# A conv + GRU kernel on one core: ScalarE copies gate biases into PSUM in place of VectorE's bias additions, and the tap shift products are issued in halves of 128 columns

## What is computed

```
x = x + (depthwise_causal_conv(x, taps = cond[:, None, :]) + b)
x = x + gru_scan(h0 = cond, inputs = x)         # 64 steps, hs stacked on the time axis
# one GRU step, h and x_t are 128 x 512, W_* are 512 x 1536
gi = x_t @ W_ih + b_ih ;  gh = h @ W_hh + b_hh  # each split in r, z, n
r = sigmoid(i_r + h_r) ;  z = sigmoid(i_z + h_z)
n = tanh(i_n + r * h_n)
h = (1 - z) * n + z * h
```

## Time and profile before

| | us |
|---|---|
| the executions shown | 1250.62 and 1250.66, median 1250.64 |
| span of the profiled execution, first to last instruction | 1249.1 |
| median less span (start and end outside the instructions) | 1.5 |
| TensorE busy | 1207.4 (97%) |
| VectorE busy | 663.6 (53%) |
| ScalarE busy | 343.1 (27%) |

### The profile page before, as it was taken

The page is one execution under the profiler, slowest core; times in us unless marked ns, Lnnn a source line. Parts: engine busy times, 40 slices in busy tenths (PEclk is TensorE's granted clock), DMA queues, the critical chain, the costliest instruction groups (busy, mean ns, idle before and its releaser), DMA issues.

```text
span 1249.1 us, 14699 instructions
## 1 busy us (share of the span) xinstructions
PE 1207.4 (97%) x5508; PEld 1019.2 (82%) x5508; DVE 663.6 (53%) x1015; ACT 343.1 (27%) x474; POOL 16.0 (1%) x20
## 2 busy tenths in 40 slices
PE   5499989999999999999999999999999999999998
PEld 5499978888888888888888888888888888888886
DVE  5255685555555455555555555555555555555554
ACT  6266661212212122212221211222121212122111
POOL 1000040000000000000000000000000000000000
PEclk9699999999999999999999999999999999999999
DMA  9996758222112222221222222122222211222200
GB/s 189 208 265 214 160 159 270 51 51 51 46 38 42 50 50 50 50 46 38 42 50 50 50 50 47 38 41 50 50 50 50 47 39 40 50 50 50 50 18 18
DMA packets 247730, 92.55 MB, mean 74 GB/s; under 512 B 203168, under 2 KB 236704, under 8 KB 246432
## 3 DMA queue, kind: packets, MB, share of 16 engines
q1 hardware_dynamic: 246848, 91.45, 31.9%
q10 hardware_dynamic: 864, 0.85, 0.3%
HBM read 58.72 MB, written 33.55 MB: 74 GB/s over the span
## 4 chain that ended last, share of the span: by engine, by line
PE 94%; DMA 4%; ACT 1%; POOL 0%; DVE 0%; SPq 0%; issue 0%; ACTq 0%; DVEq 0%
PE bank L715 83%; PE bank L695 9%; DMA x_sb<-in_x_dram 4%; PE bank L704 2%; ACT w_ih_hi L513 1%; ACT w_hh_hi L513 0%; POOL w_hh_lo L297 0%; DVE stage L578 0%; SPq L328 0%; DVE h_less_n L646 0%; DVE h L648 0%; DVE pre_z L640 0%; ACTq L317 0%; SPq L312 0%; ACT xT_hi L505 0%
## 5 line engine op out<-in xcount | busy, mean ns | idle before, releaser
L715 PE MATMUL bank<-w_ih_hi,xT_hi 128*128 128x512 f32 x768 | 305.5, 398 | 1.3 <-DVE w_ih_lo L297 1.1
L715 PE MATMUL bank<-w_hh_hi,hT_hi 128*128 128x512 f32 x768 | 298.9, 389 | 1.2 <-DVE w_hh_lo L297 0.8
L715 PE MATMUL bank<-w_ih_hi,xT_lo 128*128 128x512 f32 x768 | 300.0, 391 | 0.0
L715 PE MATMUL bank<-w_ih_lo,xT_hi 128*128 128x512 f32 x768 | 299.3, 390 | 0.0
L715 PE MATMUL bank<-w_hh_hi,hT_lo 128*128 128x512 f32 x768 | 298.8, 389 | 0.0
L715 PE MATMUL bank<-w_hh_lo,hT_hi 128*128 128x512 f32 x768 | 298.8, 389 | 0.0
L715 PEld LDWEIGHTS bank<-w_hh_hi,hT_hi 128*128 128x128 f32 x768 | 144.2, 188 | 31.8 <-issue 1.9
L715 PEld LDWEIGHTS bank<-w_ih_hi,xT_hi 128*128 128x128 f32 x768 | 144.3, 188 | 30.9 <-POOL w_ih_lo L297 1.0
L715 PEld LDWEIGHTS bank<-w_ih_hi,xT_lo 128*128 128x128 f32 x768 | 144.1, 188 | 31.0
L715 PEld LDWEIGHTS bank<-w_hh_hi,hT_lo 128*128 128x128 f32 x768 | 144.2, 188 | 29.9
L715 PEld LDWEIGHTS bank<-w_hh_lo,hT_hi 128*128 128x128 f32 x768 | 144.2, 188 | 29.9
(11 more groups left out here) (54 smaller groups left out, 796.6 us busy)
## 6 DMA issues: line engine op xcount, KB each, us to landing
xt<-xres SPq DMA_DIRECT2D x128, 128.0 KB, 2.6
out_dram<-out_t SPq DMA_DIRECT2D x64, 256.0 KB, 2.1
x_quads<-xres SPq DMA_DIRECT2D x252, 64.0 KB, 2.4
x_sb<-in_x_dram SPq DMA_DIRECT2D x2, 4096.0 KB, 35.3
xres<-kept SPq DMA_DIRECT2D x4, 1920.0 KB, 9.1
x_sb<-in_x_dram SPq DMA_DIRECT2D x2, 3072.0 KB, 37.8
xres<-stage SPq DMA_DIRECT2D x4, 1024.0 KB, 9.2
xres<-stage SPq DMA_DIRECT2D x2, 2048.0 KB, 8.1
```

The costliest lines, as they stand in the source:

```text
L715: mm = nc.tensor.matmul(psum[:, :], a[:, rows], w[which][:, cols], start=start and n == 0, stop=stop and n == 2)
```

## The change

It has two parts that don't touch each other.

The tap shift products are issued as two matmuls of 128 columns each where there was one of 256, so 256 in all. The start flag is on the first of the four of a shift, the stop flag on the last.

In the GRU steps ScalarE writes a gate's bias into its PSUM bank with a copy (`put_bias`) as soon as the bank's content was read, and all later products add onto it (no start flag). The sigmoids read PSUM directly, and VectorE reads `ps_hn` and `ps_in` directly. The four bias additions of VectorE remain for the first step alone, in place in PSUM (`add_first_bias`). TensorE waits for `bias_r_put`, `bias_in_put`, `bias_z_put` and (new) `bias_hn_put`. ScalarE's first round is now written out too.

```diff
             def step(i, u):                                   # ScalarE
...
-                act.wait_ge(pre_r_ready, t + 1)
-                nc.scalar.activation(r[:, :], pre_r[:, :], ACT.Sigmoid).then_inc(r_ready, 1)
+                act.wait_ge(gh_r_done, t + 1)
+                if first(i, u):
+                    act.wait_ge(first_bias_added, 2)
+                nc.scalar.activation(r[:, :], ps_r[:, :], ACT.Sigmoid).then_inc(r_ready, 1)
+                if not last(i, u):
+                    act.wait_ge(r_ready, t + 1)
+                    put_bias(ps_r, bias_rz[:, R:R + D], bias_r_put)
                 act.wait_ge(pre_n_ready, t + 1)
                 nc.scalar.activation(n_gate[:, :], pre_n[:, :], ACT.Tanh).then_inc(n_ready, 1)
-                act.wait_ge(pre_z_ready, t + 1)
-                nc.scalar.activation(z[:, :], pre_z[:, :], ACT.Sigmoid).then_inc(z_ready, 1)
                 if not last(i, u):
+                    put_bias(ps_in, bias_ih[:, N:NG], bias_in_put)
+                act.wait_ge(gh_z_done, t + 1)
+                if first(i, u):
+                    act.wait_ge(first_bias_added, 4)
+                nc.scalar.activation(z[:, :], ps_z[:, :], ACT.Sigmoid).then_inc(z_ready, 1)
+                if not last(i, u):
+                    act.wait_ge(z_ready, t + 1)
+                    put_bias(ps_z, bias_rz[:, Z:Z + D], bias_z_put)
+                    put_bias(ps_hn, bias_hh[:, N:NG], bias_hn_put)
                     act.wait_ge(hT_done, t + 2)
...
+            def put_bias(psum, bias, done):
+                nc.scalar.activation(psum[:, :], bias, ACT.Copy).then_inc(done, 1)
...
-            rounds(act, False, step)
+            rounds(act, True, step)
                                                               # VectorE
-                dve.wait_ge(gi_done, t + 1)
-                nc.vector.tensor_tensor(new_x[:, :], ps_in[:, :], bias_ih[:, N:NG], ALU.add).then_inc(new_x_ready, 1)
+                    dve.wait_ge(gi_done, 1)                   # first step only
+                    add_first_bias(ps_in, bias_ih[:, N:NG])
...
-                dve.wait_ge(gh_r_done, t + 1)
-                nc.vector.tensor_tensor(pre_r[:, :], ps_r[:, :], bias_rz[:, R:R + D], ALU.add).then_inc(pre_r_ready, 1)
+                    dve.wait_ge(gh_r_done, 1)                 # first step only
+                    add_first_bias(ps_r, bias_rz[:, R:R + D])
+                    dve.wait_ge(gh_n_done, 1)
+                    add_first_bias(ps_hn, bias_hh[:, N:NG])
+                    dve.wait_ge(first_bias_added, 3)
                 dve.wait_ge(gh_n_done, t + 1)
-                nc.vector.tensor_tensor(new_h[:, :], ps_hn[:, :], bias_hh[:, N:NG], ALU.add).then_inc(new_h_ready, 1)
-                dve.wait_ge(new_h_ready, t + 1)
                 dve.wait_ge(r_ready, t + 1)
-                nc.vector.tensor_tensor(reset_h[:, :], new_h[:, :], r[:, :], ALU.mult).then_inc(reset_h_ready, 1)
+                nc.vector.tensor_tensor(reset_h[:, :], ps_hn[:, :], r[:, :], ALU.mult).then_inc(reset_h_ready, 1)
                 dve.wait_ge(reset_h_ready, t + 1)
-                nc.vector.tensor_tensor(pre_n[:, :], reset_h[:, :], new_x[:, :], ALU.add).then_inc(pre_n_ready, 1)
+                nc.vector.tensor_tensor(pre_n[:, :], ps_in[:, :], reset_h[:, :], ALU.add).then_inc(pre_n_ready, 1)
                 if first(i, u):
                     dve.wait_ge(bias_rz_ready, 2)
-                dve.wait_ge(gh_z_done, t + 1)
-                nc.vector.tensor_tensor(pre_z[:, :], ps_z[:, :], bias_rz[:, Z:Z + D], ALU.add).then_inc(pre_z_ready, 1)
+                    dve.wait_ge(gh_z_done, 1)
+                    add_first_bias(ps_z, bias_rz[:, Z:Z + D])
...
+            def add_first_bias(psum, bias):
+                nc.vector.tensor_tensor(psum[:, :], psum[:, :], bias, ALU.add).then_inc(first_bias_added, 1)
                                                               # TensorE
                 for part in (taps_hi, taps_lo):
-                    mm = nc.tensor.matmul(bank[u % 8][:, 0:CH * P], window[:, u:u + P], part[:, :],
-                                          start=part is taps_hi, stop=part is taps_lo)
+                    for c in range(CH):
+                        mm = nc.tensor.matmul(bank[u % 8][:, c * P:(c + 1) * P], window[:, u:u + P],
+                                              part[:, c * P:(c + 1) * P],
+                                              start=part is taps_hi and c == 0,
+                                              stop=part is taps_lo and c == CH - 1, skip_group_check=True)
...
-                return product(psum, xT_hi, xT_lo, 0, gate, True, stop)
+                return product(psum, xT_hi, xT_lo, 0, gate, False, stop)
...
-                h_product(ps_hn, N, True).then_inc(gh_n_done, 1)
+                if not first(i, u):
+                    pe.wait_ge(bias_hn_put, t)
+                h_product(ps_hn, N, first(i, u)).then_inc(gh_n_done, 1)
...
-                    pe.wait_ge(pre_r_ready, t + 1)
+                    pe.wait_ge(bias_r_put, t + 1)
                     x_product(ps_r, R, False)
-                    pe.wait_ge(new_x_ready, t + 1)
+                    pe.wait_ge(bias_in_put, t + 1)
                     x_product(ps_in, N, True)
                     pe.wait_ge(h_ready, t + 1)
                     transpose(ps_hT, hT_done, h_block)
-                    pe.wait_ge(pre_z_ready, t + 1)
+                    pe.wait_ge(bias_z_put, t + 1)
                     x_product(ps_z, Z, False).then_inc(gi_done, 1)
```

More of the change, by code:

```diff
@@ L161, in conv_residual_gru @@
     out_t0, out_t1 = place("out_t0", D), place("out_t1", D)
-    pre_r, pre_z, r, z, n_gate = (place(n, D) for n in ("pre_r", "pre_z", "r", "z", "n_gate"))
-    new_h, new_x, reset_h, pre_n = (place(n, D) for n in ("new_h", "new_x", "reset_h", "pre_n"))
+    r, z, n_gate = (place(n, D) for n in ("r", "z", "n_gate"))
+    reset_h, pre_n = (place(n, D) for n in ("reset_h", "pre_n"))
     h_less_n = place("h_less_n", D)
@@ L239, in conv_residual_gru @@
         gh_z_done = sem("gh_z_done")
-        new_x_ready = sem("new_x_ready")
-        pre_r_ready = sem("pre_r_ready")
+        first_bias_added = sem("first_bias_added")
+        bias_r_put, bias_z_put, bias_in_put, bias_hn_put = (sem(f"bias_{g}_put") for g in ("r", "z", "in", "hn"))
         r_ready = sem("r_ready")
-        new_h_ready = sem("new_h_ready")
         reset_h_ready = sem("reset_h_ready")
@@ L247, in conv_residual_gru @@
         h_less_n_ready = sem("h_less_n_ready")
-        pre_z_ready = sem("pre_z_ready")
         z_ready = sem("z_ready")
@@ L715, in block_product @@
                     mm = nc.tensor.matmul(psum[:, :], a[:, rows], w[which][:, cols],
-                                          start=start and n == 0, stop=stop and n == 2)
+                                          start=start and n == 0, stop=stop and n == 2, skip_group_check=True)
                 return mm
```

## The result

The kernel after takes 1270.28 us (median of 1269.82 and 1270.73) against 1250.64: a ratio of 1.0154, interval 1.0137 to 1.0171. It is slower by 19.6 us, or 1.5%: more than the interval allows for chance, and less than 2%. The profiled execution has a span of 1268.6 us, 19.5 us more than before.

What follows compares the result with a forecast made beforehand. TensorE was taken to bound the kernel (busy 97%), except in the head, set by the load of `x_sb`. Span 1249.1 + 21.0 + 1.0 - 0.7 = 1270.4, with 1.5 outside 1271.9 us; 8-in-10 range 1249.5 to 1276.

Steps and rivals of the forecast that it cites:

- the slow split: Shift products in the head: short products some 0.227 us apart delay the convolution, +21.0 us; the forecast case, chance 0.60.
- Steps at 16.80 us, nothing for the copies and waits: The 63 later GRU steps: ScalarE's bias copies arrive in time, tightest 2.5 us to spare at `ps_in`; cost 0.
- Split, +21.0: Head: 256 short shift products outlast the load of x, so the convolution starts at 68.6 instead of 47.64, +21.0 us.
- the 0.220 of the convolution's records: Head: alternative spacing for the short shift products, 0.220 us throughout, convolution at 65.3, +17.6 us; not taken.
- The hidden rival: Head: short products keep one pass, 0.06 to 0.12 us apart, and end within the load; 1250.9 us, chance 0.30.
- First step, +1.0 with bounds 0.9 and 1.7: First GRU step: TensorE's product of x with r now waits for sigmoid and bias copy, +1.0 us.
- End, -0.7: End of the kernel: `pre_z` leaves the chain before sigmoid `z`, -0.7 us.
- Full fp32 cost: Head: two records and 0.44 us per short shift product, convolution at 121.4, +73.7 us, 1324.6 us; chance 0.05.
- puts late: GRU steps: bias copies over 3.1 us would delay each step, or contention costs up to 7 us; chance 0.05.

Runs made afterwards that it cites:

- put_7: bias_only with ScalarE's copy of the n bias into `ps_in` made seven times in a row in each GRU step; 1339.27 us.
- whole_lead: The kernel before with the first 16 shifts left whole (256 columns) and the other 48 cut in halves of 128; 1252.09 us.
- put_3: bias_only with ScalarE's copy of the n bias into `ps_in` made three times in a row in each GRU step; 1253.3 us.
- split_only: The kernel before with only the shift products cut into halves of 128 columns, the GRU as before; 1266.84 us, ratio 1.0119.
- moving_64: split_only with only 64 of the 128 moving columns of each half from the ninth shift on, stationary operand whole; 1266.84 us.
- weights_64: split_only with a stationary operand of 64 columns instead of 128 from the ninth shift on; 1250.42 us.
- bias_only: The kernel after with the shift products whole (256 columns), so only the GRU bias change remains; 1254.68 us, ratio 1.0024.
- table_early: bias_only with a one-column sigmoid ahead of ScalarE's waits in the first GRU step; 1253.19 us, ratio 1.0009.

## Why the prediction was right or wrong

The time (1271.9 forecast, 1270.3 measured) was right, and the case (the slow split) too. That the number came out so close is luck: the head was put 4.9 us too high and the first step 3.2 us too low, and the two errors nearly cancelled.

- **Steps at 16.80 us, nothing for the copies and waits: right.** The copies take 0.59 to 0.60 us (0.63 taken), and 2.6 us were to spare at `ps_in` (2.5 worked out). `put_7` shows that the spare time was read from the right wait.
- **Split, +21.0: the step that failed is "as if the short product were done in four passes over its columns", with 8 products at 0.427 and 247 at 0.227 us.** Measured +16.1, and a different mechanism. The spacing of a short product goes with its stationary columns, 0.214 us at half clock and 0.112 at full, with no extra passes, and at half clock the whole stream ran. The prediction let the clock rise after 3.4 us, as it had for the whole products, and didn't ask whether a stream of short ones raises it too. Why the clock did not rise is open. The value passed over for it, the 0.220 of the convolution's records, would have given +17.6, nearer by luck: those are bound differently, since they don't change with the clock.
- **The hidden rival** had the cost at full clock right (0.112 and 0.115 us measured, 0.11 from the transposes). With the clock up it is what happens: `whole_lead` is hidden. What it lacked was the clock. The sentence in the prediction's list against it, "nothing but that the trace has no such product", left out that the shift products of the same trace began at 1.2 GHz, so that the short ones would have to see the clock rise as well.
- **First step, +1.0 with bounds 0.9 and 1.7: wrong.** The kernel after's trace shows 2.45 us of stop and 1.7 of half clock, 4.2. The step that failed is "ScalarE's peeled first round only saves two table loads there, off the chain". One load stays, and it now stands behind the wait for VectorE, while before it ran from 181.55, during that wait. The bound from above counted no clock at all; `put_3` shows that the fall doesn't come every time.
- **End, -0.7: right.**
- **Full fp32 cost, puts late:** out, by 0.115 us a product at full clock and by 16.80 us steps.

The Trainium skill (TensorE: Matmul & The Clock Gate, section LDWEIGHTS (loading the stationary operand)) gives the load of weights as the stationary columns divided by 1.2, in ns, 107 for 128 columns. The 0.112 and 0.115 us measured at full clock are within 8% of it; the 0.214 at half clock is twice as much, so here the load goes with the granted clock.

## What to carry to other kernels

In these runs the spacing of a stream of fp32r matmuls was the larger of two prices, one by its moving columns and one by its stationary ones, and cutting products short adds the second for each piece: before cutting, compare the piece's columns with the stationary ones at both clock levels. Idle time ahead of a late DMA hides such a cost only up to a threshold, so work out that threshold (here 0.151 us a product) and check that the clock you count on is really granted in that stretch. When a wait is put in front of an engine's instruction, look at what the instruction brings with it: here a table load moved behind the wait and lengthened TensorE's stop by about its 1.28 us. In three of the four traces with that stop half clock followed, which cost the kernel after another 1.7 us.

## What the runs showed of the hardware that was not expected

- A steady stream of products can leave TensorE's clock low: 256 fp32r products of 128 columns, back to back for 55 us, stayed at 1.2 GHz (`split_only`, `moving_64`, the kernel after). It rose during the convolution's stream that followed (records at 383 ns by 72 us). The same short products kept 2.4 GHz for 21 us once it was granted (`whole_lead`).
- With a stationary operand of 64 columns the same number of moving columns ran 0.107 us apart and the clock rose after some 5 us (`weights_64`).
- The length of a stop did not decide whether half clock followed. After stops of 2.45 us (the kernel after), 2.25 (`bias_only`) and 2.20 (the first step of `put_7`) it did, after 2.44 us in `put_3` it didn't, and neither after 1.2 us, once (`table_early`) or in every step (`put_7`). Between its halves the convolution stops for 1.3 us in either kernel: the kernel before keeps its clock there, the kernel after falls to half, which costs nothing, as the fp32 records take 0.220 us at either clock. The windows behind that stop, before and then after:

```profile
106.00:108.00 2.00, 2.00 (x11) 2.00 (x11) 2.00 (x4) 0.38 (x1) 0.00 (x0) 1.00 0.00 0
```

```profile
122.00:124.00 2.00, 2.00 (x10) 2.00 (x10) 2.00 (x4) 0.52 (x1) 0.00 (x0) 0.54 0.00 0
```

- The granted clock column reads 1.00 ahead of the first change in a profile, also where the spacings say one half; durations of a known form (430 against 383 ns for the convolution's records) tell the two apart.
